# First attention of a graph kernel: sums kept in PSUM and taken out per block by ScalarE, one-hots made by VectorE, gathers released four slots at a time

## The reference

```python
h = relu(layernorm(x))
feat = (h @ W1).reshape(n, 8, 64)
e = leaky_relu(el[src] + er[dst], 0.2)
m = segment_max(e, dst)
ex = exp(e - m[dst])
denom = segment_sum(ex, dst)
out = segment_sum((ex / denom[dst])[:, :, None] * feat[src], dst)
x = elu(out.reshape(n, 512))
```

## Time and profile before

| | us |
|---|---|
| runs shown (median of 3) | 3218.97 |
| lowest, highest | 3212.55, 3219.84 |
| the profiled execution, its own time | 3221.76 |
| its span in the trace | 3218.8 |

### The profile page before, as it was taken

The page is one execution under the profiler, slowest core; times in us unless marked ns, Lnnn a source line. Parts: engine busy times, 40 slices in busy tenths (PEclk is TensorE's granted clock), DMA queues, the critical chain, the costliest instruction groups (busy, mean ns, idle before and its releaser), DMA issues.

```text
span 3218.8 us, 51543 instructions
## 1 busy us (share of the span) xinstructions
PE 2639.7 (82%) x18059; PEld 1978.5 (61%) x18059; DVE 2334.0 (73%) x3121; ACT 1279.2 (40%) x3089; POOL 999.5 (31%) x1235
## 2 busy tenths in 40 slices
PE   4777777999899998886888987777676777866999
PEld 2666665545455555785777776555555555765888
DVE  7999997797334444987777878866666666785786
ACT  6888885020001112003444444444444444403343
POOL 3000000111102223006666666666666664003000
PEclk8999999999999999997999999998889889967999
DMA  4444446434478783215666776666676666052453
GB/s 136 185 171 179 170 180 236 137 115 132 138 241 260 254 261 108 86 50 176 190 186 192 194 196 176 181 188 183 182 188 181 188 183 170 24 182 61 155 164 108
DMA packets 311101, 538.20 MB, mean 167 GB/s; under 512 B 108482, under 2 KB 213460, under 8 KB 310596
## 3 DMA queue, kind: packets, MB, share of 16 engines
q1 hardware_dynamic: 241700, 309.63, 29.3%
q0 software_dynamic: 69152, 225.28, 24.9%
HBM read 420.89 MB, written 115.11 MB: 167 GB/s over the span
## 4 chain that ended last, share of the span: by engine, by line
PE 56%; DVE 27%; issue 5%; ACT 5%; another core or an unknown queue 4%; DMA 2%; POOL 1%; DVEq 0%; SPq 0%; ACTq 0%; POOLq 0%
PE ps L1715 22%; PE ps L1496 14%; PE ps L1703 9%; DVE a L586 8%; PE ps L1632 5%; DVE a L581 3%; DVE a L582 3%; PE ps L1400 2%; DVE a L1158 2%; DVE a L830 1%; ACT oht L1365 1%; PE ps L1630 1%; ACT oh L1367 1%; PE ps L1522 1%
## 5 line engine op out<-in xcount | busy, mean ns | idle before, releaser
L1715 PE MATMUL ps<-a,oh 128*128 128x260 f32 x2008 | 510.8, 408 | 148.8 <-ACT oh L1367 56.9
L1824 POOL DMA_INDIRECT a<-t,mid x502 | 482.5, 961 | 443.6 <-DVE cin L940 167.8
L1365 ACT ACTIVATE oht<-iota,mid 128x128 f32<-128x128 f32 x830 | 333.3, 402 | 639.3 <-PE ps L1715 425.4
L1496 PE MATMUL ps<-a 128*128 128x512 f32 x1200 | 554.4, 602 | 13.2 <-DVE a L763 13.2
L1715 PEld LDWEIGHTS ps<-a,oh 128*128 128x128 f32 x2008 | 390.3, 202 | 251.0 <-ACT oh L1367 110.2
L1158 DVE TENSOR_TENSOR a<-a,ps 128x520 f32 x415 | 286.6, 691 | 286.8 <-PE ps L1715 196.0
L1715 PE MATMUL ps<-wts,oh 128*128 128x260 f32 x1312 | 345.7, 419 | 97.5 <-DVE wts L1170 40.1
L1463 PE MATMUL ps<-a 128*128 128x200 bf16 x1568 | 319.9, 255 | 108.7 <-issue 53.3
L1824 POOL DMA_INDIRECT wts<-t,mid x328 | 312.5, 953 | 187.5 <-issue 79.4
L1715 PEld LDWEIGHTS ps<-wts,oh 128*128 128x128 f32 x1312 | 265.3, 209 | 165.3 <-ACT oh L1367 59.8
L1496 PEld LDWEIGHTS ps<-a 128*128 128x128 f32 x1200 | 218.6, 192 | 220.8 <-issue 214.6
(11 more groups left out here) (327 smaller groups left out, 3920.6 us busy)
## 6 DMA issues: line engine op xcount, KB each, us to landing
a<-at_d SPq DMA_DIRECT2D x60, 1280.0 KB, 6.1
at_d<-a SPq DMA_DIRECT2D x49, 800.0 KB, 3.3
mt_d<-a SPq DMA_DIRECT2D x49, 800.0 KB, 4.9
a<-mt_d SPq DMA_DIRECT2D x30, 1280.0 KB, 6.1
a<-trlo_d SPq DMA_DIRECT2D x49, 512.0 KB
ot_d<-a SPq DMA_DIRECT2D x49, 320.0 KB, 6.0
a<-ot_d SPq DMA_DIRECT2D x49, 256.0 KB, 3.3
a<-t,mid POOLq DMA_INDIRECT x502
```

Of the source, the lines that this page charges most:

```text
L1365: e.activation(oht[:, k, :], iota[:, :], ACT.Abs, bias=ndl[:, k, s:s + 1]).then_inc(*own.inc())
L1496: m = e.matmul(acc[f].rearrange("p (x d) -> p x d", x=8), X[:, hi, P * f:P * (f + 1)], a, start=(hi == 0), stop=end, skip_group_check=True)
L1715: t = e.matmul(pbig[b][:, 512 * u:512 * u + 260], oh[:, so, k, :], hrows[2 * r + k][:, 260 * u:260 * (u + 1)], start=(k == 0), stop=(k == 1))
L1824: e.indirect_dma_start(out=hrows[2 * r + k], out_offset=None, in_=t2, in_offset=bass.IndirectOffsetOnAxis(ap=srci[:, k, s:s + 1], axis=0)) ...
```

## The change

- PSUM sums. The matmuls of a slot add to what stands in PSUM (`start=False`) over all slots of a block; such a sequence is a **run**. Two pieces of PSUM are used in turn, the third is left for the lookups. Which piece a slot uses PE reads from a table (`acc_at`), and which run it belongs to from another (`acc_lim`), for four slots at a time.
- ScalarE takes a run out to `acc1` when `head_mm` says that its last slot is done (`run_end`), and prepares the piece for the run after next: zeros in the first phase, the block's sums so far in the second.
- There are 50 runs: the 25 blocks over the slots below 178 (S0), then the 25 blocks over the slots from 178 on. Blocks without slots in a phase have runs without slots, which are taken out and prepared as well. `exps(1)` stands between the two phases.
- VectorE makes the one-hots, by one comparison with iota for each half, ten slots deep (`ohs`), and no longer adds. It takes a lookup out three slots after PE's instead of two.
- GpSimd waits once for the buffers of four slots, and no longer clears `acc1` (nor does VectorE).
- Small operations are added to VectorE's preparation in the first convolution (`run_endf`, `run_no`, `acc_lim`, `acc_at`), a load of SyncE's (`msmall`) waits for the last slot, and the second half's numerators are written at slot 186 in SyncE's order, not 188.

```diff
@@ scalar @@
-            for s in range(NS):
-                so = s % 4
-                for k in range(2):
...
-                    e.activation(oht[:, k, :], iota[:, :], ACT.Abs, bias=ndl[:, k, s:s + 1]).then_inc(*own.inc())
-                    e.wait_ge(*own.last())
-                    e.activation(oh[:, so, k, :], oht[:, k, :], ACT.Relu, bias=1.0, scale=-1.0).then_inc(head_oh, 1)
-                if s == MARK["less max", 1] + 4:
+            def prepare(r):
+                phase, b = divmod(r, NB)
+                i = acc1[:, W1 * b:W1 * (b + 1)].rearrange("p (u w) -> p u w", u=2) if phase else bc(mzero[:, :].rearrange("p (a b) -> p a b", a=1), [P, 2, W1 // 2])
+                e.activation(run_sum(r), i, ACT.Copy).then_inc(acc_ready, 1)
...
+            for r in range(RUNS):
+                if r % 4 == 0:
+                    e.load(run_regs, run_end[0:1, r:r + 4])
+                e.reg_alu(run_at, run_regs[r % 4], 1, ALU.max)
+                e.wait_ge(head_mm, run_at)
+                b = r % NB
+                e.activation(acc1[:, W1 * b:W1 * (b + 1)].rearrange("p (u w) -> p u w", u=2), run_sum(r), ACT.Copy).then_inc(acc_out, 1)
+                if r + 2 < RUNS:
+                    e.wait_ge(acc_out, r + 1)
+                    prepare(r + 2)
+                if r == NB - 1:
                     exps(1)
@@ tensor @@
+                e.reg_alu(lim, lim_regs[s % 4], 1, ALU.max)
+                e.wait_ge(acc_ready, lim)
                 e.wait_ge(head_oh, 2 * s + 2)
                 e.wait_ge(head_mul, s + 1)
-                e.wait_ge(*(V("found", 8, before[1]) if before[0] == "look" else (head_add, before[1] + 1)))
+                c = e.snap(col_regs[s % 4], donate=True, min_val=0, max_val=1024)
                 for u in range(2):
                     for k in range(2):
-                        t = e.matmul(pbig[b][:, 512 * u:512 * u + 260], oh[:, so, k, :], hrows[2 * r + k][:, 260 * u:260 * (u + 1)],
-                                     start=(k == 0), stop=(k == 1))
+                        t = e.matmul(ps[:, 512 * u:512 * u + 2048][:, bass.ds(c, 260)], ohs[so][:, k, :], hrows[2 * r + k][:, 260 * u:260 * (u + 1)],
+                                     start=False, stop=True, skip_group_check=True)
                 t.then_inc(head_mm, 1)
@@ vector @@
-                e.tensor_tensor(d, d, pbig[RING["slot", s][0]].rearrange("p (u w) -> p u w", u=2)[:, :, 0:260], ALU.add).then_inc(head_add, 1)
...
+                if s >= RO:
+                    e.wait_ge(head_mm, s - RO + 1)
+                for k in range(2):
+                    e.tensor_scalar(ohs[so][:, k, :], iota[:, :], ndl[:, k, s:s + 1], None, ALU.is_equal).then_inc(head_oh, 1)
...
-                if s >= 2:
-                    add_heads(s - 2)
-                    for i in AFTER.get(s - 2, ()):
-                        found_b(i)
+                for i in AFTER.get(s - LOOK_LAG, ()) if s >= LOOK_LAG else ():
+                    found_b(i)
@@ lookups' places @@
+            u_ = i_ % 3 if i_ < LOOKS_A + len(AFTER[-1]) else 2
@@ gpsimd @@
-                if s >= NR:
-                    e.wait_ge(head_mm, s - NR + 1)
+                if s >= NR and (s - NR) % 4 == 0:
+                    e.wait_ge(head_mm, min(s - NR + 4, NS - NR))
```

More of the change, by code:

```diff
@@ L37 @@
 W1 = 520
+RO = 10
+S0 = 178
+RUNS = 2 * NB
 OT = {8: 3, 1: 4}
@@ L342, in program @@
         hrows = [t[:, W1 * k:W1 * (k + 1)] for t in hpair for k in range(2)]
+        run_no = small[0:4, 128:256]
+        ohs = [oh[:, i, :, :] for i in range(4)] + [a4[:, 544 + 256 * i:800 + 256 * i].rearrange("p (k n) -> p k n", k=2) for i in range(RO - 4)]
         foundb = [t.rearrange("p b w -> p (b w)")[:, 0:128] for t in (stat[:, :, :], den[:, :, :])]
@@ L686, in job @@
                     plan(8, 4, NC, 336, 67, "plan2")
+                    e.tensor_scalar(run_endf[:, 0:NB - 1], small[0:1, 65:64 + NB], float(S0), None, ALU.min).then_inc(*V.inc())
+                    e.tensor_copy(run_endf[:, NB:2 * NB - 1], small[0:1, 65:64 + NB]).then_inc(*V.inc())
+                    e.memset(run_endf[:, NB - 1:NB], float(S0)).then_inc(*V.inc())
+                    e.memset(run_endf[:, 2 * NB - 1:64], float(NS)).then_inc(*V.inc())
+                    e.wait_ge(*V.last())
+                    e.tensor_copy(run_end[:, :], run_endf[:, :]).then_inc(*V.inc("run ends"))
                 elif kind == "turned":
@@ L719, in job @@
                     e.wait_ge(pe_prep, PREP[name])
[L720 removed]
+                    e.tensor_copy(ndl[:, name[1], :], mp[1][:, :]).then_inc(*V.inc(name))
                 elif kind == "slots2":
                     e.wait_ge(pe_prep, PREP["slots2"])
[L723 removed]
+                    e.tensor_scalar(run_no[:, :], slot_no[:, :], float(S0), float(NB), ALU.is_ge, ALU.mult).then_inc(*V.inc())
+                    e.wait_ge(*V.last())
+                    e.scalar_tensor_tensor(out=run_no[:, :], in0=run_no[:, :], scalar=1.0, in1=mp[1][0:4, 0:P], op0=ALU.add, op1=ALU.add).then_inc(*V.inc())
                     e.tensor_copy(cr[:, :], mp[1][0:4, P:2 * P]).then_inc(*V.inc("slots2"))
+                    e.wait_ge(*V.last())
+                    e.tensor_copy(acc_lim[:, :], run_no[:, :]).then_inc(*V.inc())
+                    e.wait_ge(*V.last())
+                    e.tensor_scalar(acc_at[:, :], acc_lim[:, :], 1, 10, ALU.bitwise_and, ALU.arith_shift_left).then_inc(*V.inc("run table"))
             def conv(number, name, o):
@@ L1225, in program @@
             AFTER.setdefault(-1 if i_ < LOOKS_A + 9 else int((i_ - LOOKS_A - 9) * 1.85), []).append(i_)
-        uses = [("look", i_) for i_ in range(LOOKS_A)] + [("look", i_) for i_ in AFTER[-1]]
-        for s_ in range(NS):
-            uses += [("slot", s_)] + [("look", i_) for i_ in AFTER.get(s_, ())]
-        RING = {use: (n_ % 3, uses[n_ - 3] if n_ >= 3 else None) for n_, use in enumerate(uses)}
+        LOOK_LAG = 3
+        RING = {}
+        for i_ in range(len(LOOKUPS[8])):
+            u_ = i_ % 3 if i_ < LOOKS_A + len(AFTER[-1]) else 2
+            before_ = [k_ for k_ in range(i_) if RING[k_][0] == u_]
+            RING[i_] = (u_, before_[-1] if before_ else None)
         MARK, SLOT = {}, [-1]
@@ L1625, in look @@
                 if before is not None:
-                    e.wait_ge(*(V("found", H, before[1]) if before[0] == "look" else (head_add, before[1] + 1)))
+                    e.wait_ge(*V("found", H, before))
                 for k in range(m):
```

83 lines of the change are left out of this document (40 added, 43 removed).

## The result

The change makes the kernel **slower**: 3272.99 us, median of 4 runs (3268.53 to 3277.29), against 3218.02 us (4 runs, 3212.55 to 3219.84). The ratio is 1.0175, with a 95% interval of 1.0158 to 1.0192. I had forecast 3111, with a range of 3062 to 3200. The profiled execution took 3268.53 us, with a span of 3266.6.

A forecast was written before the change was run, and what follows sets the result against it. No engine is full in the plain slots, so a loop of waits around PE's late signals was taken as the bound. Savings of 42.5, 8 and 57.4, together 108 from 3221.8, gave 3114, less 3: 3111 us; range 3062 to 3200.

The forecast's parts named there:

- the part on POOL: Gathers in plain slots: with users of PE's signals further away, POOL's own pace rules, 2.50 us a slot, taken as 2.55.
- Stage A, -42.5: The 162 slots with lookups between them: 2.75 us each, 445.5 us instead of 488.
- Stage B, -8: The 19 slots with the last sweeps: 4.4 us less VectorE work and most of its 4.9 us idle gone.
- The stop, 33 us: At slot 178: PE stands while ScalarE handles 24 pairs of runs, 28 us, plus exponentials and signals.
- Restart of POOL, 37.6 us after slot 177: POOL's next group of gathers (slots 186 on) waits for slot 179: 33 + 3.6 + 1 us.
- Stage C, -57.4: Plain slots from slot 177: 37.6 to POOL's restart, 584 for 229 slots, 8 to finish; 629.6 us instead of 687.
- One-hots, 0.23 us: VectorE's new one-hots, two a slot: about 0.23 us each at 128 columns, from other tensor-scalar rows.
- Registers on PE at 0: PE's register-addressed targets: 0.07 us at most a slot, 0 beside other work.
- the forecast's own bounds: Whole kernel 3070 to 3165 us: slots with lookups at 2.63 to 2.9, plain slots at 2.50 to 2.7; chance 0.68.
- Late signals still rule: Rival, slots: PE's signals stay above 15 us late in the loop and groups of four add waiting; 3201 us, chance 0.16.
- The lookups' single buffer: Rival, slots with lookups: each lookup waits for VectorE's maximum, 7.0 us for two slots; 3225 us, chance 0.06.
- One-hots hold up the gathers: Rival, both slot stages: each gather waits out one-hots, 0.23 to 0.46 us; 3255 us at 3.0 a slot, chance 0.10.

The follow-up runs named there:

- 3217 kind: Chips on which the unchanged kernel took 3217 and 3200 us (two chips); the main result belongs here by its times.
- c_before: The kernel before, unchanged, traced on the 3217 kind chip that also ran the changed kernel: 3216.39 us, ratio 1.0002.
- 3009 kind: Chips on which the unchanged kernel took 3008 to 3009 us (four chips).

## Why the prediction was wrong

The rates of a slot, all versions side by side, us:

| | with lookups (A) | plain (C) |
|---|---|---|
| forecast | 2.75 | 2.55 |
| 3217 kind: before (c_before) | 3.04 | 2.90 |
| changed | 3.27 | 2.90 |
| changed, no loads of exponentials | 3.23 | 2.87 |
| one phase, wait per slot | 3.07 | 2.91 |
| the same with constant targets (3200) | 3.08 | 2.85 |
| 3009 kind: before with grouped wait | 2.56 | 2.51 |
| changed | 2.56 | 2.51 |
| one phase, no gathers | 2.55 | 1.75 |

**The step that failed** is the one in the part on POOL: that PE's late signals are a delay which deeper buffers ride over, "so stage C becomes POOL's". I took the lateness of 4 to 7 us for something in the loop of waits. The chip that ran both kernels tells otherwise. PE's waits in 2130 to 2700, the kernel before, then the changed one:

```profile
PE ps L1715 <- ACT oh L1367: 61.4, 26, 4.1
...
PE ps L1715 <- DVE a L1170: 37.8, 13, 3.9
PE ps L1715 <- DVE wts L1170: 33.8, 13, 3.8
...
PE ps L1715 <- issue: 30.0, 17, 3.6
```

```profile
PE ps L1744 <- issue: 151.3, 86, 3.1
PE ps L1744 <- DVE a L1170: 0.5, 1, 0.5
PE ps L1744 <- DVE oh L1170: 0.5, 1, 0.5
```

Before, PE stood 133.0 us for ScalarE and VectorE and 30.0 for nobody, 163 together; now it stands 1.0 us for others and 151.3 for nobody, 152 together. The change did take the waits away. Idle time with no releaser came into their place, all but 11 us of it, and these went to PE's own work (407.46 us busy before, 416.91 now, at a granted clock of 0.91 and 0.83). The rate of a slot stayed at 2.90. I read it so: whatever makes PE slow there sets the pace by itself, and the waits of before were how the others met it. Five programs of this kind of chip, with different waits, all run plain slots at 2.85 to 2.91 us. PE's share of a slot (2.16 us busy in stage C, and 159.4 us idle in the 650 us of its waits, 0.72 a slot) is 2.88 us of the 2.94, so deeper buffers have next to nothing left to take away. The label "issue" alone doesn't prove a slow stretch: on the 3009 kind the kernel before with the grouped wait has 59.1 us of it in 500 us, but in 127 pieces of at most 0.8 us.

The 3009 kind says the same from the other side. There the forecast rates hold: 2.51 for 2.55 plain, and 2.56 for 2.75 with lookups. But the kernel before runs at them as well (with the grouped wait, the form in which it was profiled there). The gain that I computed was the distance between two kinds of chip, and no part of the change bridges it.

Point by point:

- *Stage A, -42.5*: measured +36. The forecast rate of 2.75 isn't reached there either on this kind (3.07 at best with the change's parts, 3.04 before). Its working was loose besides: a lookup after every 1.85 slots is 0.54 of one a slot and not half, so 1.81 + 0.89 = 2.70 at full clock; where PE keeps up it is 2.56. What I didn't price in this stage at all is the grouped wait: 31.8 us, by the only difference between the two programs up to there. I had checked the grouping only for POOL's own pace ("17.5 us before"), where it does hold: 6 us on the 3009 kind. With PE behind, POOL stands until four slots are done and then has to refill; that is how I explain the 32 us, and the waits of POOL above fit it.
- *Stage B, -8*: measured -7.
- *The stop, 33 us*: 31.07, with 1.16 us a pair exactly as taken. This term was right in place, cause and size, and it alone is over half of the 57 us by which the stages grew.
- *Restart of POOL, 37.6 us after slot 177*: its next gather starts at 2108.60, 36.9 us after 2071.71, where slot 177 ends.
- *Stage C, -57.4*: from slot 177 on it takes 31 + 17 + 667 = 715 us instead of 687, so +28, which is the stop and nothing else.
- *One-hots, 0.23 us*: 0.30 from start to end of one, but they overlap, and two take 0.47 to 0.48 us together: 0.24 each, as taken. These groups of stage C (2103 to 2787) show the first, with the gathers beside them, and the timeline from 2445 to 2447 the second:

```profile
L1854 POOL DMA_INDIRECT a<-t,mid x274 | 259.6, 947 | 133.3 <-issue 78.6 <-remote 47.7 <-PE ps L1744 7.0
...
L1170 DVE TENSOR_SCALAR a<-iota,mid 128x128 f32<-128x128 f32 x272 | 68.1, 299 | 0.0
```

```profile
2445.75 0.95 POOL L1854 DMA_INDIRECT a<-t,mid  x1 [0.30 <-issue]
2445.96 0.47 DVE L1170 TENSOR_SCALAR oh<-iota,mid 128x128 f32<-128x128 f32 x2
```

- *Registers on PE at 0*: borne out where it was tried alone, on the 3009 kind, at C 2.51 with and without them.
- *Smaller slips of the working*: the forecast's own bounds (A at 2.63 with C at 2.50, A at 2.9 with C at 2.7) give 3079 and 3169, not 3070 and 3165; the single buffer's 7.0 us for two slots is 3.49 each, not 3.45, which makes that rival 3231. Neither changes the verdict.

The rivals. *Late signals still rule* (0.16) was the nearest: it gave stage C no gain. It took the rate there as 2.80, where it is 2.94, and gave stage A a gain of 10, so it came to 3201 and not to 3273. My reason against it, that the users of the signals now stand seven to ten slots away, is what fell. *The lookups' single buffer* (0.06) shows in the waits: in 1486 to 2010 VectorE waits 42 times, up to 5.7 us, before a maximum (L874), and PE before the lookups (L1647) for the maxima.

```profile
DVE stat L874 <- remote: 73.0, 20, 5.1
DVE den L874 <- remote: 72.7, 22, 5.7
...
PE ps L1647 <- DVE den L874: 29.9, 17, 5.1
```

But the version with the wait per slot has the same single buffer and takes 3.07 us a slot, against 3.04 before. So with all else that the change does there, the single piece loses 0.03 us a slot net, 5 us; the rest was the grouped wait. *One-hots hold up the gathers* (0.10) is false: a gather takes 947 and 948 ns in stage C, 945 before in 2130 to 2700, with two one-hots in every slot, and the gather of 2445.75 takes 0.95 us with both one-hots inside it. The Trainium skill (SBUF — State Buffer, "SBUF: two separate sides") has a VectorE operation in a mode that uses both ports, its example an fp32 tensor_copy from SBUF to SBUF, keep GpSimd from writing descriptors. If the one-hots ran in such a mode, which no row here tells, these gathers should have lengthened, and they didn't.

The chances were mis-set in one way. I named no cause for the lateness, and wrote that "the signals are PE's and the change does nothing about them"; I still gave 0.68 to its doing no harm. What a trace doesn't explain should have been the likeliest thing to stay.

**What stays open.** First, why PE is slow on the 3217 kind. It isn't mainly the loads of exponentials, nor the register instructions. The gathers of rows are suspected, since the two kinds differ where these run and hardly elsewhere: the changed kernel's slots with lookups begin at 1486 us on the one and 1484 on the other, and what follows the last slots takes 480 us against 462, while the part between takes 1301 against 1084. In the 450 us from 2800 on of the changed kernel's trace on the 3217 kind, without these gathers, PE's matmuls of the second attention (L1720) don't appear among the waits for nobody, and their weight loads with 4.2 us; the lookups there (L1649) do, with 10.2 us, but with 12.5 us on the 3009 kind too. But the runs with half the bytes and with no gathers, which would tell, only came on chips that have no slow stretches; that the gathers cause them is argued and not shown. Second, the grouped wait alone in the kernel before, and the wait per slot with two phases, never ran on the 3217 kind; the split of 31.8 and 27.1 us is read from two traces, not from a run of each. So it could be that grouping costs that much only together with the lookups' single piece of PSUM. Third, whether a kind belongs to the chip or to a state that the chip was in: each chip was seen in one group of runs only.

## What to carry to other kernels

An engine's lateness that no row explains is itself a candidate for the bound. A change that only moves its users further away should then be priced at no gain, until a trace shows the engine keeping up; here the waits vanished and nearly as much idle time without a releaser came instead. A wait for several buffers at once is cheap only while the releasing engine keeps up: here 6 us where PE did, 32 (read from two traces) where it was late. And where an in-order engine has housekeeping once per block, count what falls due at one place: fifty short operations, harmless when spread, stopped the kernel for 31 us at a phase boundary, and one phase instead of two removed that.

## What the hardware showed that I had not expected

- The same kernel takes 3008 to 3009 us on four chips, and 3200 and 3217 on two others. Plain slots take 2.51 against 2.90 us there, slots with lookups 2.56 against 3.04 (the first of each with the grouped wait).
- On the second kind, about every 24 us in the plain slots of the changed kernel, PE issues a weight load only every 1.6 to 3.3 us for 6 to 10 us, in the middle of a slot with all its inputs there, then catches up.
- TensorE's granted clock is 0.83 in stage C of the changed kernel and 0.91 in that of the kernel before, with PE busy 74% and 72% of the time, and 1.00 in the same stage on the other kind, with 80%. So the busy share alone doesn't set it.
- In PE's stop of 31 us the granted clock is 0.56 on average, near the lower level of 1.2 GHz, and in the 17 us of work behind it 0.90; the lower clock outlasts the stop by a few us.
- The gathers took 0.95 us each on either kind of chip in the plain slots. Only the pauses between them differ: 0.30 us, and on the 3217 kind the waits for PE besides.
